# Reordering the hand-over between two layers, and splitting the last row statistics into four pieces

## What is computed

```python
xn = layernorm(x)                                  # layer 0
x  = x + attention(xn, Wq, Wk, Wv, Wo)             # 16 heads of 64, rotary, causal softmax
       + int8_linear(xn, weight_int8, scale, bias) # one scale from max|xn| over all batches
xn = layernorm(x)                                  # layer 1
left, right = xn @ compare_left, xn @ compare_right          # K = 64
c  = left @ right.T / sqrt(256)                              # 512 x 512 per batch
x  = x + ((c > threshold) * softmax(c + gate_bias)) @ xn
       + sigmoid(xr @ W_r) * (relu(xk @ W_k)**2 @ W_v)       # xr, xk: each row mixed with the row before it
```

## Time and profile before

| | before |
|---|---|
| three runs, median (lowest to highest) | 1073.49 us (1069.6 to 1074.68) |
| the profiled execution, its own time | 1067.62 us |
| the span in that profile | 1065.5 us |
| mean granted TensorE clock | 0.998 of full |
| PE busy | 1015.0 us (95%) |
| DVE busy | 838.4 us (79%) |
| ACT busy | 741.9 us (70%) |
| POOL busy | 767.7 us (72%) |
| chain that ended last | PE 71%, DVE 15%, ACT 7%, issue 4%, POOL 2% |

### The profile page before, as it was taken

The page is one execution under the profiler, slowest core; times in us unless marked ns, Lnnn a source line. Parts: engine busy times, 40 slices in busy tenths (PEclk is TensorE's granted clock), DMA queues, the critical chain, the costliest instruction groups (busy, mean ns, idle before and its releaser), DMA issues.

```text
span 1065.5 us, 24181 instructions
## 1 busy us (share of the span) xinstructions
PE 1015.0 (95%) x8486; PEld 704.4 (66%) x8486; DVE 838.4 (79%) x1760; ACT 741.9 (70%) x2014; POOL 767.7 (72%) x941
## 2 busy tenths in 40 slices
PE   5879999999999999999999999999999978989998
PEld 4556665666666666666666666666666755767676
DVE  7988889777778888877777777777777756888885
ACT  5978886666666666666666666666666765989994
POOL 3766668767777787877786777677877545868884
PEclk9999999999999999999999999999999999999999
DMA  8633444333433333333333233433333100000011
GB/s 280 216 97 105 141 127 138 90 119 102 119 108 96 109 99 90 90 110 95 91 99 115 90 91 99 120 90 90 90 91 95 46 1 1 21 22 21 22 39 41
DMA packets 99703, 98.73 MB, mean 93 GB/s; under 512 B 13312, under 2 KB 95360, under 8 KB 98944
## 3 DMA queue, kind: packets, MB, share of 16 engines
q1 hardware_dynamic: 99584, 97.19, 29.9%
HBM read 56.25 MB, written 40.90 MB: 91 GB/s over the span
## 4 chain that ended last, share of the span: by engine, by line
PE 71%; DVE 15%; ACT 7%; issue 4%; POOL 2%; DMA 0%; ACTq 0%; DVEq 0%; POOLq 0%
PE bank L1637 22%; PE bank L1721 12%; PE bank L1735 12%; PE bank L1752 8%; PE bank L1708 6%; PE bank L1709 5%; PE bank L1710 2%; PE bank L1927 2%; ACT arena L868 1%; PE bank L1873 1%; POOL arena L627 1%; DVE arena L1514 1%; DVE nm L1361 1%; DVE arena L1376 1%; DVE arena L1339 1%
## 5 line engine op out<-in xcount | busy, mean ns | idle before, releaser
L627 POOL TENSOR_SCALAR arena<-arena,rc 128x128 f32<-128x128 f32 (+3 forms) x512 | 276.6, 559 | 207.9 <-DVE rc L1369 207.8
L868 ACT ACTIVATE arena<-bank,nm 128x256 f32<-128x256 f32 (+3 forms) x512 | 268.3, 526 | 79.8 <-DVE nm L1361 70.1
L1361 DVE TENSOR_REDUCE nm<-bank 128x1 f32<-128x256 f32 (+3 forms) x512 | 230.8, 481 | 91.7 <-PE bank L1710 88.5
L1721 PE MATMUL bank<-ident,arena 128*128 128x128 f32 x1280 | 216.8, 277 | 14.9 <-DVE arena L1376 12.0
L1721 PEld LDWEIGHTS bank<-ident,arena 128*128 128x128 f32 x1280 | 144.3, 141 | 52.4 <-DVE arena L1376 29.1
L876 ACT ACTIVATE arena<-bank 128x512 f32<-128x512 f32 (+3 forms) x256 | 111.4, 435 | 77.7 <-PE bank L1721 77.4
L1709 PE MATMUL bank<-arena 128*128 128x256 f16 (+3 forms) x512 | 153.1, 299 | 0.0
L1735 PE MATMUL bank<-arena 128*64 128x512 f32 (+3 forms) x1024 | 152.0, 439 | 0.0
L1708 PE MATMUL bank<-arena 128*128 128x256 f16 (+3 forms) x512 | 147.2, 300 | 2.2 <-DMA arena<-scr 1.8
L1376 DVE COPY arena<-bank 128x512 f32<-128x512 f32 (+3 forms) x256 | 124.3, 486 | 22.6 <-PE bank L1721 18.4
L1735 PEld LDWEIGHTS bank<-arena 128*64 128x64 f32 x1024 | 67.8, 136 | 94.3 <-issue 73.3
(11 more groups left out here) (174 smaller groups left out, 2289.9 us busy)
## 6 DMA issues: line engine op xcount, KB each, us to landing
arena<-scr SPq DMA_DIRECT2D x320, 128.0 KB, 2.7
scr<-arena SPq DMA_DIRECT2D x256, 128.0 KB, 1.7
arena<-in_weights SPq DMA_DIRECT2D x5, 1024.0 KB, 7.1
x_sb<-in_x SPq DMA_DIRECT2D x8, 512.0 KB, 8.4
out<-x_sb SPq DMA_DIRECT2D x16, 256.0 KB, 2.2
xscr<-arena SPq DMA_DIRECT2D x12, 256.0 KB, 2.9
xsh<-xscr SPq DMA_DIRECT2D x6, 256.0 KB, 3.4
xsl<-xscr SPq DMA_DIRECT2D x6, 256.0 KB, 3.7
```

The source lines that it names most:

```text
L627: last = pool.tensor_scalar(pr[slot][:, OFF[i]:OFF[i + 1]], pr[slot][:, OFF[i]:OFF[i + 1]], rc[:, slot, i:i + 1], 1.0, ALU.mult, ALU.mult)
L868: act.activation(pr[slot][:, OFF[i]:OFF[i + 1]], s_tile[i], ACT.Exp, bias=nm[:, slot, i:i + 1], accum_out=sm[:, slot, i:i + 1]).then_inc(e ...
L1361: dve.tensor_reduce(nm[:, slot, i:i + 1], s_tile[i], AX.X, ALU.max, negate=True).then_inc(max_done, 1)
L1721: last = pe.transpose(banks[5 + h][:, (i - j) * P:(i - j + 1) * P], pr[2 * par + h][:, OFF[i] + j * P:OFF[i] + (j + 1) * P], ident[:])
```

## The change

Three orders are changed; no instruction is added, removed or altered, and no wait.

- DVE and POOL, hand-over: the scaling of the first half of batch 7's integer product, `ffn_part(7, 0)`, goes ahead of the two `xt_low3(0, .)`, and POOL's `add_ffn(7, 0)` ahead of the first two `mix_before`. The two `side_low(0, .)` go behind `ffn_part(7, 1)` and the first two `mix_all`.
- PE, hand-over: of the portions of the second half, `attended(7, 1)`, two instead of four precede the comparison of batch 0, and six instead of four follow it.
- DVE, second layer: the statistics of batches 6 and 7 and their root stood together between the bodies 0 and 1. Now the statistics of batch 6 stand behind body -1, those of batch 7 behind body 0, parts 0 and 1 of the root behind body 1, and parts 2 and 3 with the bias behind body 2.

```diff
@@ POOL
             pool.wait_ge(xf3_zero, 1)
+            add_ffn(NB - 1, 0)
             mix_before(0, 0)
             mix_before(0, 1)
-            for h in range(2):
-                add_ffn(NB - 1, h)
+            add_ffn(NB - 1, 1)
             mix_before(0, 2)
@@ DVE
+            ffn_part(NB - 1, 0, wo)
             xt_low3(0, 0)
             xt_low3(0, 1)
-            ffn_part(NB - 1, 0, wo)
-            side_low(0, 0)
-            side_low(0, 1)
             ffn_part(NB - 1, 1, pj)
             mix_all(0, 0)
             mix_all(0, 1)
+            side_low(0, 0)
+            side_low(0, 1)
             top(0, 0, 0)
             mix_all(0, 2)
             residual(NB - 1, 0, wo)
             residual(NB - 1, 1, pj)
-            body3(-1, 1)
-            body3(0, 0)
-            for b in range(NB - 2, NB):
-                row_statistics(b)
-            roots(slice((NB - 2) * NT, NB * NT), 3)
-            roots_bias(slice((NB - 2) * NT, NB * NT))
-            for n in range(1, NB):
+            last_two = slice((NB - 2) * NT, NB * NT)
+            for n in range(-1, NB):
                 body3(n, n % 2)
+                if n < 1:
+                    row_statistics(NB - 1 + n)
+                elif n < 3:
+                    roots(last_two, 3, (2 * n - 2, 2 * n - 1))
+                if n == 2:
+                    roots_bias(last_two)
@@ PE
             attended(NB - 1, 0, (4, 5, 6, 7), wo)
-            attended(NB - 1, 1, (0, 1, 2, 3), pj)
+            attended(NB - 1, 1, (0, 1), pj)
             compare(0, 0, (lrl_done, 2, 0, 0))
             compare(0, 1, (lrl_done, 2, 0, 1))
-            attended(NB - 1, 1, (4, 5, 6, 7), pj)
+            attended(NB - 1, 1, (2, 3, 4, 5, 6, 7), pj)
```

## The result

| | before | changed |
|---|---|---|
| first measurement, median (lowest to highest) | 1073.44 us (1069.6 to 1074.68, 4 runs) | 1060.79 us (1060.29 to 1061.62, 4 runs) |
| measured again | 1072.43 us (8 runs) | 1061.6 us (1060.54 to 1062.0, 5 runs) |
| a third time | 1071.7 us (13 runs) | 1060.48 us (1060.36 to 1062.09, 5 runs) |
| profiled execution, first measurement: own time / span | 1067.62 / 1065.5 us | 1060.55 / 1058.8 us |

The ratios are 0.9889 (95% interval 0.9867 to 0.9911), 0.9899 (0.9886 to 0.9913) and 0.9896 (0.9877 to 0.9914): the change makes the kernel about 1.05% faster, 11 us. The prediction said 8.3 us less and 1065.2 us, with a range from 1061.0.

The account below looks back on a forecast made before the run. PE, busy 95% of the span, was taken as the bound, with gains only in its waits and low clock. Hand-over 4.89 plus statistics 3.4 gave 8.3 us off 1073.49, hence 1065.2 us; range 1061 to 1070.1.

Parts of the forecast that it names:

- The first wait and what covers it: Hand-over: `ffn_part(7, 0)` put first runs 3.72 us earlier, covered by idle DVE time; PE begins `attended` at 873.70.
- the new wait in front of `sides`: Hand-over, PE: `sides(0, 0)` needs `xt_low3(0, 1)`, a wait of 0.51 us that was hidden behind `ffn_part` before.
- What follows on PE: Hand-over, PE's work from `attended` to `gated(0, 0)`: moves by 4.89 us if nothing else stops PE.
- The slack of the comparison: Hand-over, comparison to exponentials: 0.5 us in front of `residual(7, 1)` and 0.75 more, as that stands ahead of `gated`.
- The rule against it: DVE's `mix_all` pair ahead of `side_low`: GpSimd's shared-port lock could stall it, making PE wait 0.4 us, 1065.6 us in all.
- Statistics: Second layer: statistics and root pieces of batches 6 and 7 fit into DVE's waits behind the bodies; gain 3.4 us.
- The clock: Hand-over, 24 `attended` matmuls: PE's clock stays at 2.4 GHz, giving back 1.68 us; bounds 0 and 1.68.
- the bound between keeping and losing the clock: PE's idleness: clock stayed at 1.00 across 3.39 us, so the bound was put between 3.39 and 4.20 us.
- The difference carried over: Whole kernel: the profiled execution's 5.87 us below the median of the runs was carried unchanged into the forecast time.

Follow-up runs that it names:

- the root in one piece: Changed kernel with the whole root and its bias behind body 1, against the changed kernel: 1061.96 us (6 runs) beside 1060.48 us (5 runs).
- both waits filled: Kernel before with unread matmuls in PE's waits, 66 in that of 4.2 us, 55 in that of 3.39 us: 1068.11 us, ratio 0.9961 against before.
- the one with the hand-over filled: Kernel before with 66 unread matmuls in PE's 4.2 us wait ahead of the first portion: 1068.71 us, ratio 0.9967 against before.
- the kernel with the hand-over alone: Kernel before with only the hand-over's three lists changed, statistics and root still together between bodies 0 and 1: 1066.08 us, ratio 0.9945.

## Why the prediction was right, and where it was not

*The first wait and what covers it: right.* `ffn_part(7, 0)` follows the memset at once, PE starts 0.84 us later, and the new wait in front of `sides` is there: 0.44 and 0.30 us. The wait alone was priced at 3.21 us and measured, with the clock taken out, at 3.29.

*What follows on PE: right in its result, too careful in its reason.* The slack of the comparison was named as 0.5 us plus 0.75, and the later place of two portions as what keeps it from becoming the bound. By the prediction's own numbers it isn't: with four portions behind it this chain ends at 889.0, which is when `gated(0, 0)` comes anyway. With the portions back at four and four nothing moved.

*The rule against it* changed nothing here. The pair `mix_all` took the same 2.42 us, and `side_low` had its slack. The port mattered in a place where I hadn't looked: the root. I priced its pieces at 0.20 us an instruction from a stretch in which POOL was idle. Behind the bodies POOL is in the middle of its `mix_low` pair (from 947.68 for 2.14 us), and the first two instructions of the piece took 0.58 and 1.01 us. POOL's timeline and DVE's:

```profile
947.68 2.14 POOL L686 TENSOR_TENSOR arena<-arena 128x512 f16<-128x512 f32 x2
...
948.22 0.58 DVE L1075 TENSOR_SCALAR nw<-mv 128x8 f32<-128x8 f32 x1
948.84 1.01 DVE L1078 TENSOR_SCALAR nw<-nw 128x8 uint32<-128x8 uint32 x1
949.88 0.17 DVE L1080 TENSOR_SCALAR nw<-nw 128x8 int32<-128x8 int32 x1
```

The piece cost 2.5 instead of 1.2 us and used up the whole wait of 2.33; the one behind body 2 cost 2.55 instead of 1.4, with 0.58 and 1.01 us for its first two as well, and left no wait either. This is the picture that the Trainium skill draws ("SBUF — State Buffer", section "SBUF: two separate sides"): the loser stands until the other's instruction is over. The trace agrees: L1075 ended at 948.80 and L1078 at 949.85, and POOL's pair at 948.75 (half of it) and 949.82; from then on all take 0.17. That section of the Trainium skill names DVE operations in a two-port mode or with two inputs in SBUF. The first two behind body 2 (L1085 and L1087) have two such inputs; L1075 and L1078 have one, and no run here shows their mode. That the first piece cost nothing was luck: the first operation of `gated(2, 0)` that PE waits for ended at 951.50, with 0.15 us from DVE to PE that is 951.65, and PE came to its transposes at 951.65. Nothing was left, as the root in one piece showed: 1.29 us longer on DVE, 1.29 us later on PE.

*Statistics: right.* 3.4 us in the sum, 3.55 in the trace, each piece off the path.

*The clock: the mechanism right, the size wrong.* The term was 1.68 us, from one execution, with 0 as its other bound. The runs put 3.6 us in its place (both waits filled; mean clock from 0.992 to 0.998), most of it in the hand-over, since filling that wait alone gave 3.0. Two steps of the working failed. The first is that "4.30 - 24 x 0.109" is what the lower clock cost in the profiled execution and was taken for what it costs: the distance from memset to gated operation, 19.44 with the clock up, was 21.11, 22.02 and 22.33 in three executions with the same wait, so 1.67, 2.58 and 2.89 us, and the last of them lost more at 900. The second is the sentence that the bound between keeping and losing the clock lies between 3.39 and 4.20 us of idleness: the same wait of 3.39 us lost it in another execution. Before's own profile had a third such wait, of 3.83 us at 64 us, which kept the clock there and lost it in the changed kernel; the prediction didn't look at it. The upper bound of the clock term was thus set from one sample, where no row allowed it.

*The difference carried over: wrong.* The profiled execution was 5.87 us below the median, and the sum carried this over unchanged to the kernel after. By the slope above, its clock of 0.998 against 0.992 stands for 6 x 0.75 = 4.5 us of it, an estimate: time that the other executions lost at 1.2 GHz. The change removes only a part of that. Before's mean of 1072.0 lies 4.4 us above its profiled execution, the changed kernel's mean of 1061.1 lies 1.8 us above the 1059.3 that the sum gave for one like it; so 2.6 us went and 1.8 stayed. What stayed can be seen in the first layer, which the change doesn't touch: before's profiled execution kept the clock behind the wait at 64 us and had the memset at 872.79, while in the eleven other profiled executions with that wait the clock fell there and the memset came at 874.26 to 876.17. So the one profile that the prediction read was untypical in two places: it lost less in the hand-over than the others with the same wait, and nothing behind the wait at 64 us. The warning was on the page: a profiled execution below the lowest timed one has to have something that the others don't, and a mean clock that near 1 says what. After the change the profiled execution (1060.55) is one of the timed ones.

The sum with the measured terms: 3.3 + 3.55 of waits and 3.6 of clock are 10.5 us; measured were 10.8 to 12.7. What of the rest is scatter and what is real isn't settled; the mean of the 14 executions of the changed kernel is 1061.1, that of the 45 of before beside the experiments 1072.0, 10.9 apart. Against the first of these two means the forecast of 1065.2 was 4.1 us too high, which is the 5.87 carried over less the 1.8 that stayed. By terms: 1.9 is the clock (3.6 in place of 1.68), 1.5 the three runs of before, whose median of 1073.49 lay above the mean of the 45, and 0.2 the waits (6.85 in place of 6.61); 0.5 is open. That the measured times came out at the edge of the range and not outside it by more is no merit of the sum: the lower end was set 4 us below it for scatter, and these terms used that up.

## What to carry to other kernels

Where PE waits in one lump for another engine, count the wait and, apart from it, the work behind it at half the clock, and take the second from many executions (their mean granted clocks stand beside their times), never from one profile. Filling the wait with idle matmuls is a cheap experiment that separates the two: it tells what the clock is worth before anything is reordered. And a lump of small operations on one engine is best cut into pieces that lie in that engine's own waits; price a piece by what the neighbours do at its new place, not by what it took at the old one.

## What the runs showed of the hardware

- The same stretch of the program with the same wait of PE in front of it loses the clock in one execution and keeps it in another: 3.39 us of idleness, kept in before's profile and in the one with the hand-over filled, lost for 3.4 us in the kernel with the hand-over alone; 3.83 us at 64 us, kept in before's profile, and at 0.50 from 68 to 72 in a later profile of the changed kernel. Of the changed kernel itself one profile has 0.57 there and two have 0.50.
- Behind the same wait of 4.20 us the hand-over lost 1.67, 2.58 and 2.89 us in three executions.
- In one execution a much shorter idleness (1.65 us) was followed by another fall, some 13 us after the clock had come back from the first. In another, with the same first fall and 1.66 us of idleness, the clock stayed up.
- Two DVE instructions on 128x8 elements took 0.58 and 1.01 us beside GpSimd's work, 0.17 us without it.
